# First and last runs of four graph layers: feature rows streamed past 32 loaded weights in four column tiles, a spread row and bounds in registers

## What is computed

```python
def reference(x, src, dst, edge_attr_16, edge_weight, ...):
    x = layernorm(x + L0(x, edge_attr_16, src, dst))    # softmax over the edges of a dst
    x = layernorm(x + L1(x, src, dst, edge_weight))     # softmax again, then an MLP of two 64-128-64 products
    x = layernorm(x + L2(x, row=src, col=dst))          # sums by src, gathers from dst, degrees as weights
    x = layernorm(x + L3(x, row=src, col=dst, value=edge_weight))
    return x

# L0, L1:  h = segment_sum(alpha[:, None] * f(x[src]), dst, num_segments=N)
# L2, L3:  h = segment_sum(weight[:, None] * x[dst], src, num_segments=N)
```

## Time and profile before

| what | value |
|---|---|
| median of 3 runs | 2804.57 us (2801.99 to 2814.03) |
| span of the profiled execution | 2797.4 us |
| mean granted clock of PE, as a share of full speed | 0.815 |
| busy: PE, DVE, POOL, ACT | 1944.0, 1685.3, 1661.4, 1497.3 us |

### The profile page before, as it was taken

The page is one execution under the profiler, slowest core; times in us unless marked ns, Lnnn a source line. Parts: engine busy times, 40 slices in busy tenths (PEclk is TensorE's granted clock), DMA queues, the critical chain, the costliest instruction groups (busy, mean ns, idle before and its releaser), DMA issues. The chain is left out here.

```text
span 2797.4 us, 27574 instructions
## 1 busy us (share of the span) xinstructions
PE 1944.0 (69%) x8422; PEld 1002.8 (36%) x8422; DVE 1685.3 (60%) x3220; ACT 1497.3 (54%) x2242; POOL 1661.4 (59%) x1610
## 2 busy tenths in 40 slices
PE   6998778679988688888999868658888875000000
PEld 3444334227643233364444327543333434000000
DVE  4876699993888578745655433997656687000002
ACT  4777667553677568746787762337777652000000
POOL 6777777600037565000777757775777768677774
PEclk9999899886999789979999996559989885555555
DMA  3233222101668674102454491442111233100002
GB/s 63 66 68 81 58 56 68 51 30 45 203 126 58 47 56 52 46 16 71 139 144 137 118 228 53 120 121 67 52 52 53 89 105 98 55 17 22 22 21 96
DMA packets 235785, 214.75 MB, mean 77 GB/s; under 512 B 156783, under 2 KB 169926, under 8 KB 235638
## 3 DMA queue, kind: packets, MB, share of 16 engines
q1 hardware_dynamic: 181190, 166.34, 20.7%
q0 software_dynamic: 51200, 46.31, 12.2%
q10 hardware_dynamic: 3248, 0.34, 0.1%
HBM read 140.36 MB, written 86.04 MB: 81 GB/s over the span
## 5 line engine op out<-in xcount | busy, mean ns | idle before, releaser
L2372 POOL DMA_INDIRECT stab<-wk,rank_i x200 | 208.5, 1042 | 289.1 <-DVE wk L588 231.4
L545 ACT ACTIVATE b_s<-ps,vec 128x512 f32<-128x512 f32 (+1 forms) x356 | 240.9, 684 | 159.4 <-PE ps L624 59.8
L2369 POOL DMA_INDIRECT u<-x2tab,dpos_i x200 | 220.8, 1104 | 82.7 <-issue 77.8
L2369 POOL DMA_INDIRECT u<-x3tab,src_i x200 | 206.1, 1030 | 85.3 <-issue 59.2
L2369 POOL DMA_INDIRECT u<-in_x_dram,src_i x200 | 201.4, 1007 | 76.7 <-issue 59.8
L2369 POOL DMA_INDIRECT e_b<-x0tab,dpos_i x72 | 72.7, 1009 | 290.9 <-DVEq L2174 265.5
L2372 POOL DMA_INDIRECT out_dram<-u,dst_i x176 | 198.2, 1126 | 74.7 <-issue 59.8
L2369 POOL DMA_INDIRECT u<-in_x_dram,dst_i x200 | 201.1, 1006 | 64.4 <-issue 59.5
L2372 POOL DMA_INDIRECT out_dram<-u,sfin_i x200 | 196.5, 982 | 66.3 <-issue 66.3
L776 DVE TENSOR_SCALAR b_x<-b_s 128x8 f32<-128x8 f32 x2 | 0.3, 168 | 389.3 <-DMA b_gl<-out_dram 389.3
L533 PE MATMUL ps<-b_h,blk_c 128*128 128x512 f32 (+1 forms) x296 | 174.4, 673 | 57.9 <-ACT b_gl L553 57.4
(11 more groups left out here) (428 smaller groups left out, 5026.4 us busy)
## 6 DMA issues: line engine op xcount, KB each, us to landing
b_gl<-in_x_dram SPq DMA_DIRECT2D x98, 256.0 KB, 2.7
wk<-dlist SPq DMA_DIRECT2D x50, 500.0 KB
wk<-slist SPq DMA_DIRECT2D x50, 500.0 KB
out_dram<-b_gl SPq DMA_DIRECT2D x93, 256.0 KB, 2.0
u<-stab SPq DMA_DIRECT2D x25, 510.0 KB
x2none<-b_gl SPq DMA_DIRECT2D x25, 250.0 KB
wk<-x2none SPq DMA_DIRECT2D x25, 240.0 KB
x2tab<-wk SPq DMA_DIRECT2D x25, 240.0 KB
```

What stands on the lines that cost most here:

```text
L545: return nc.scalar.activation(b_s[l][:, 0:w], pB[l][:, 0:w], ACT.Abs_reciprocal_sqrt, bias=col(EPSV))
L2369: pool.indirect_dma_start(out=o, out_offset=None, in_=tab, in_offset=at_ix(ix), **kw).then_inc(s, 16)
L2372: pool.indirect_dma_start(out=tab, out_offset=at_ix(ix), in_=a, in_offset=None, bounds_check=rows_n - 1, oob_is_err=False).then_inc(s, 16)
```

## The change

**Sums.** The operands change places. `hw` is now what is loaded: the four columns of the eight blocks of a group, 32 columns, and the 512 feature columns of that group stream past them. The result is 32 x 512, of which only an eighth is wanted (columns of `hw` of a block against features of the same block). Four groups make a chunk: their four matmuls write the partitions 0, 32, 64 and 96 of one PSUM bank, `e0` and `e1` in turn. There are 7 chunks, the last of one group. For each chunk DVE multiplies the bank by a mask of the wanted blocks (`mask8`), reduces the eight blocks to one (into `q_b`), PE transposes that (L1454 of the changed kernel), and DVE copies it out and gives the bank back. So a layer has 25 matmuls of 512 streamed columns and 7 transposes on PE, and 21 instructions of DVE more, in place of 100 or 200 matmuls; the scan now runs over one piece in layer 1 too and its copies out of PSUM fall away. In layer 0 columns 2 and 3 of `hw` are set to zero. In layer 3 chunk c waits for the gathers of its last groups.

**Spread row.** `x0tab` gets 1024 rows behind row E in place of one, all filled with the bias row, and the index of a source without an incoming edge becomes E + 8p, where p is the partition of the index's place in the layout in which the indices are made.

**Bounds.** The two bounds of POOL's DMAs are put in registers once.

Two semaphores are merged into others, with their counts (`list_st`, `consts`).

```diff
+    NONE = 8
-    x0tab, ... = (dram(n, (r, D)) for n, r in (("x0tab", E + 1), ...))
+    x0tab, ... = (dram(n, (r, D)) for n, r in (("x0tab", E + 128 * NONE), ...))
...
-        e_a, e_b, e_c, e_d, q_a, q_b = (sb(n, [128, 512]) for n in ("e_a", "e_b", "e_c", "e_d", "q_a", "q_b"))
+        e_a, e_d, q_a, q_b = (sb(n, [128, 512]) for n in ("e_a", "e_d", "q_a", "q_b"))
+        e_bc = sb("e_bc", [128, 1024])
+        e_b, e_c = e_bc[:, 0:512], e_bc[:, 512:1024]
...
         def ends_unit(layer, after, **deps):
-            us = (.14 if layer < 2 else .23) * GC
...
+            text = []
+            for c in CHUNKS:
+                b = f"e{c % 2}"
+                text += [f"p{c} pe 1.6 +{b}" + (f" <p{c - 1}" if c else ""), f"m{c} dve .7 <p{c}", f"r{c} dve .7 <m{c}",
+                         f"x{c} pe .3 <r{c}", f"y{c} dve .25 -{b} <x{c}"]
+            text += ["scan dve {}".format((2.9, 5.0, 2.3, 2.3)[layer]), "t pe 1 +e1", "copy dve .5 -e1"]
+            unit(("lay", layer), 0, ";".join(text), after, **deps)
...
+            if m == 0:
+                nc.vector.memset(hw[0:P, :, 2:4], 0.0)
...
         def ends_pe(pe, t, layer):
-            def block(b):
-                return nc.tensor.matmul(e0[0:D, k * b:k * b + k], a[0:P, b, :], hw[0:P, b, 0:k], start=True, stop=True)
-            def pair(b):
...
+            a = (xs, xs, rdst, rdst)[layer]
+            for c in CHUNKS:
+                yield t[f"p{c}"]
+                bank_c, name = chunk_bank(c)
                 pe.wait_ge(S("weights"), layer + 1)
+                pe.wait_ge(S(name + "_free"), use(name, t[f"p{c}"]))
+                if layer == 3:
+                    for g in chunk_groups(c)[-2:]:
+                        pe.wait_ge(*gathered(3, g))
+                for q, g in enumerate(chunk_groups(c)):
+                    last_e = nc.tensor.matmul(bank_c[32 * q:32 * q + 32, :],
+                                              hw[0:P, GC * g:GC * g + GC, :].rearrange("p b k -> p (b k)"),
+                                              a[0:P, GC * g:GC * g + GC, :], start=True, stop=True)
                 last_e.then_inc(S("ends_ps"), 1)
+        def ends_rows_pe(pe, t, layer):
+            for c in CHUNKS:
+                yield t[f"x{c}"]
+                r = 32 * len(chunk_groups(c))
+                pe.wait_ge(S("ends_red"), len(CHUNKS) * layer + c + 1)
+                nc.tensor.transpose(chunk_bank(c)[0][0:D, 0:r], q_b[0:r, D * c:D * c + D], ident[0:r, 0:r]).then_inc(S("ends_t"), 1)
+        def ends_mask_dve(dve, t, layer):
+            for c in CHUNKS:
+                yield t[f"m{c}"]
...
+                product = (q_a, e_d)[c % 2]
+                k = stepped(nc.vector.tensor_tensor(t3(product[0:r, :]), t3(chunk_bank(c)[0][0:r, :]), bc(mask8[0:r, :], D), ALU.mult))
+                yield t[f"r{c}"]
+                dve.wait_ge(S("dve_step"), k)
+                nc.vector.tensor_reduce(q_b[0:r, D * c:D * c + D], product[0:r, :].rearrange("p (b d) -> p d b", b=GC), AX.X,
+                                        ALU.add).then_inc(S("ends_red"), 1)
+        def ends_copy_dve(dve, t, layer):
...
+                dve.wait_ge(S("ends_t"), len(CHUNKS) * layer + c + 1)
+                nc.vector.tensor_copy(ends_sums(layer)[0:D, 32 * k * c:32 * k * c + n * k].rearrange("d (b k) -> d b k", k=k),
+                                      bank_c[0:D, 0:4 * n].rearrange("d (b k) -> d b k", k=4)[:, :, 0:k]).then_inc(S(name + "_free"), 1)
...
-            stt(addr, addr, -float(E), valid, ALU.add, ALU.mult)
-            ts(addr, addr, float(E), None, ALU.add)
+            none_row = sgn[:, 15:16]
+            ts(none_row, X["io"][:, 0:1], NONE / 128.0, float(E), ALU.mult, ALU.add)
+            stt(addr, addr, none_row, valid, ALU.subtract, ALU.mult)
+            ts(addr, addr, none_row, None, ALU.add)
...
-            sp.dma_start(x0tab[E:E + 1, :], rowc[0:1, R_B0, :]).then_inc(S("x0_none"), 16)
+            sp.dma_start(x0tab[E:E + 128 * NONE, :].rearrange("(p s) d -> p s d", s=NONE),
+                         rowc[:, R_B0, :].unsqueeze(1).broadcast_to((128, NONE, D))).then_inc(
+                S("x0_none"), 16)
...
+            last_edge, last_node = pool.to_reg(E - 1), pool.to_reg(N - 1)
-            def gather(o, tab, ix, s, rows_n=None):
-                kw = {} if rows_n is None else dict(bounds_check=rows_n - 1, oob_is_err=False)
+            def gather(o, tab, ix, s, last=None):
+                kw = {} if last is None else dict(bounds_check=last, oob_is_err=False)
...
+            fours = stepped(nc.vector.tensor_reduce(wpn[:, 0:32], ident[:, :].rearrange("p (a k) -> p a k", k=4), AX.X, ALU.add))
+            dve.wait_ge(S("dve_step"), fours)
+            nc.vector.tensor_reduce(mask8[:, :], wpn[:, 0:32].rearrange("p (g b) -> p b g", b=GC), AX.X, ALU.add)
```

More of the change, by code:

```diff
@@ L49, in gnn_resnorm_kernel @@
         dram(n, (FLAT,)) for n in ("q_spos", "q_ddeg", "q_dps", "q_sdeg", "q_dpos", "q_rank"))
-    x0tab, x2tab, x2none, x3tab = (dram(n, (r, D)) for n, r in (("x0tab", E + 1), ("x2tab", E), ("x2none", E), ("x3tab", E)))
+    x0tab, x2tab, x2none, x3tab = (dram(n, (r, D)) for n, r in (("x0tab", E + 128 * NONE), ("x2tab", E), ("x2none", E), ("x3tab", E)))
     stab = dram("stab", (E, RW))
@@ L1415, in softmax_dve, with chunk_bank, chunk_groups @@
             dve.drain().then_inc(S("weights"), 1)
+        def chunk_bank(c):
+            return (e0, e1)[c % 2], f"e{c % 2}"
+        def chunk_groups(c):
+            return range(4 * c, min(4 * c + 4, NG))
         def ends_pe(pe, t, layer):
-            a, k = (xs, xs, rdst, rdst)[layer], (2, 4, 2, 2)[layer]
-            def block(b):
-                return nc.tensor.matmul(e0[0:D, k * b:k * b + k], a[0:P, b, :], hw[0:P, b, 0:k], start=True, stop=True)
-            def pair(b):
-                o, c = (e1, b - QB) if k == 4 and b >= QB else (e0, b)
-                return nc.tensor.matmul(o[:, k * c:k * c + 2 * k], xs[0:P, b:b + 2, :].rearrange("p b d -> p (b d)"),
-                                        hw[0:P, b:b + 2, 0:k], start=True, stop=True)
@@ new lines, in ends_copy_dve @@
+        def ends_copy_dve(dve, t, layer):
+            k = 4 if layer == 1 else 2
+            for c in CHUNKS:
+                yield t[f"y{c}"]
+                n = GC * len(chunk_groups(c))
+                bank_c, name = chunk_bank(c)
+                dve.wait_ge(S("ends_t"), len(CHUNKS) * layer + c + 1)
+                nc.vector.tensor_copy(ends_sums(layer)[0:D, 32 * k * c:32 * k * c + n * k].rearrange("d (b k) -> d b k", k=k),
+                                      bank_c[0:D, 0:4 * n].rearrange("d (b k) -> d b k", k=4)[:, :, 0:k]).then_inc(S(name + "_free"), 1)
@@ L2412, in _ @@
                 for k in range(GC):
-                    scatter(stab, E, rank_i[:, GC * g + k:GC * g + k + 1], rec[g % 2][:, RW * k:RW * k + RW], S(f"placed{g % 2}"))
+                    scatter(stab, last_edge, rank_i[:, GC * g + k:GC * g + k + 1], rec[g % 2][:, RW * k:RW * k + RW], S(f"placed{g % 2}"))
             pool.wait_ge(S("x2_st"), 32 * NG)
@@ L2429, in _ @@
                 for b in range(GC * g, GC * g + GC):
-                    gather(rdst[:, b, :], x3tab, spos_i[:, b:b + 1], gathered(3, g)[0], E)
+                    gather(rdst[:, b, :], x3tab, spos_i[:, b:b + 1], gathered(3, g)[0], last_edge)
             for l in LANES:
@@ L2444, in _ @@
                         rows, ix = rdst[:, b, :] if g >= STAGED else staged(g)[:, D * k:D * k + D], fidx_i
-                    scatter(out, N, ix[:, b:b + 1], rows, S("final_st"))
+                    scatter(out, last_node, ix[:, b:b + 1], rows, S("final_st"))
         @block.tensor
@@ L2453, in _ @@
             pe_programs += [softmax_pe(pe, at["sm", m], m) for m in range(2)]
-            pe_programs += [ends_pe(pe, at["lay", layer], layer) for layer in range(4)]
+            pe_programs += [p(pe, at["lay", layer], layer) for p in (ends_pe, ends_rows_pe) for layer in range(4)]
             pe_programs += [carry_pe(pe, at["lay", layer], layer) for layer in range(4)]
@@ L2501, in _ @@
             dve_programs += [softmax_dve(dve, at["sm", m], m) for m in range(2)]
-            dve_programs += [carry_dve(dve, at["lay", layer], layer) for layer in range(4)]
+            dve_programs += [p(dve, at["lay", layer], layer) for p in (ends_mask_dve, ends_copy_dve, carry_dve) for layer in range(4)]
             dve_programs += [prep2_dve(dve, at["prep2", k], k) for k in range(2)]
```

90 lines of the change are left out of this document (26 added, 64 removed).

## The result

The changed kernel takes **2760.57 us** (median of 4 runs, 2747.97 to 2764.01) against 2803.28 us of the kernel before beside it: a ratio of 0.9835 with a 95% interval of 0.9806 to 0.9863. The forecast was 2765, range 2705 to 2825. The profiled execution has a span of 2760.7 us against 2797.4, so -36.7 us. The sum came out near the forecast (-36.7 us for -40); several of its terms did not.

What follows compares the result with a forecast made beforehand. POOL's gathers and scatters bound the kernel from 1326 us on, PE and its chain before that. Terms -8 -12 +4 -5 -11 -6 -2 sum to -40 us, a span of 2757; with 7.2 for the median, 2765 us, range 2705 to 2825.

Steps and rivals of the forecast that it cites:

- stab scatters: First stab scatter to x2tab gathers: second record stands 17 DVE instructions behind the first instead of 13, POOL waits; +4 us.
- Layer 0's sums: Layer 0's sums up to the x0tab gathers: cheaper chunks against more dense work and PE waits; -8 us (-13 to +11).
- x0tab to second softmax: First x0tab gather to second softmax: spread row quickens gathers, added dense work refills the room; 381 to 365 us, -16.
- PE reaches 92 to 96% where it leads: x0tab gathers to second softmax: 343 us of PE work divided by 0.94 gives 365 us.
- Layer 1: Second softmax to first stab scatter: softmax +7, sums -8, way to the first record +5 us.
- Layer 2 and the x3tab gathers: Layer 2: shorter sums before the store POOL waits for, -5 us; x3tab gathers: less DVE time beside them, -2 us.
- The own wait: POOL's 14.5 us gap inside the last scatters falls to about 4, as dense blocks before layer 3's last sums leave; -11.
- The next scatters: 89 scatters in the 139.6 us after that gap: four dense blocks leave, about a quarter of the DVE time; -6 us.
- Registers: Bounds of POOL's DMAs: 1000 register moves go, but they were hidden; 0 us (bounds 0 and -38).
- The slow one: Rival, chance 0.15: column tiles run one after another at PE's low clock, 93 us more, total 2858.
- More than that: Rival, chance 0.20: register moves cost 0.04 us each (-38), or x0tab stretch falls by 46 us at full clock; about 2730.
- The dense blocks eat the gain: Rival, chance 0.18: x0tab stretch stays at 381 us, softmax and first record take upper prices; 2793 us, no change.

Runs made afterwards that it cites:

- the long hold: Changed kernel with no new dense block started from the first x0tab gather to layer 1's second group: 2635.37 us, ratio 0.9421.
- the short hold: Changed kernel with no new dense block started between the second softmax and layer 1's second group: 2721.74 us, ratio 0.9723.

## Why the prediction was right, and where its steps were not

The total was right partly by luck, since errors cancel: the sums of layers 0 and 1 gave 25 us more than forecast, and the x0tab stretch, the way to the first record, the stab scatters and the last scatters came out 32 us worse. The 7.2 us added for the median over the span did not come either: the median, 2760.57 us, lies at the span of the profiled execution, 2760.7.

- **Layer 0's sums** (-8, measured -21.6). The chunk was right (1.00 us for 1.2), the transposes too (2.0 us for 2.1). Two other terms were mis-sized. The 4 us charged for PE's waits on DVE did not come: PE is busy 22.65 of 22.80 us, the dense matmuls between the chunks cover the chain through DVE. And the other work, reckoned as 4.5 us as before plus 15.8 us, took 13.3 us in the first row of the table, with PE's busy time in the second about as before (122.91 against 123.80): two dense matmuls there had cost 3.8 us at the low clock, and now all run at the full one, where one behind another of its shape takes 0.86 us and not the 1.10 us priced. The clock was in the prediction, but only as a sign to look for, not as a term. The price of a tile change, put at nothing, is about 0.1 us each and is part of the 1.00 us of a chunk.
- **x0tab to second softmax** (-16, measured -9.7). The mechanism was right on both sides: the row gives 25 to 33 us, and the refill takes some 24 us of it back. The step that failed is "PE reaches 92 to 96% where it leads": it was busy 328.30 of 373.4 us, 88%, and the work itself was 15 us less than the 343 us reckoned. The run with the long hold shows what the dense blocks cost there: 105 us of PE's busy time went (328.30 to 223.21), and with it 98 us of the stretch.
- **Layer 1** (softmax +7, sums -8, first record +5; measured +4.4, -19.4, +13.5). The sums are the same error as in layer 0. The first record was charged by DVE instructions, up to +12; the hold showed that the dense blocks which start in softmax and sums are the cause.
- **stab scatters** (+4, bounds 0 to +8; measured +15.8). Right in place, too small: the second record alone costs 9 us (20.4 us behind the first, 11.4 before), the rest of the scatters 3 us, and the start of the x2tab gathers another 3.
- **Layer 2 and the x3tab gathers** (-5 and -2; -4.2 and -3.3): right in size. Layer 2's sums fell from 45.5 to 24.4 us, most of it hidden by POOL's gathers; the wait fell by 9.2 us, from 21.5 to 12.3, but the x2tab gathers ahead of it took 289.4 us instead of 284.4. In the run with the bounds as numbers, of the same order, they took 284.8, so these 5 us may be scatter between runs. In the x3tab gathers the mechanism is the one named: DVE's busy time fell from 160.79 to 132.55 us, the gathers above 1.1 us from 18 to 12, and POOL's busy time from 206.09 to 202.95 us.
- **The own wait** (-11, measured -12.7): right, and so is its reason: the last sums now end at 2180.7 us, 3.5 us after POOL's last x3tab gather, where they had ended 15 us after it.
- **The next scatters** (-6, measured -0.7). This step failed. DVE's busy time did fall (113.54 to 89.96 us, as the earlier trace rows and the last row of the table show), but 88 scatters kept POOL busy for 115.05 us, where 89 had for 112.74. POOL and DVE side by side in the changed kernel:

```profile
2282.88 1.25 POOL L2385 DMA_INDIRECT out_dram<-u,dst_i  x1 [0.30 <-issue]
2284.39 1.19 DVE L988 TENSOR_TENSOR wk<-wk,vcs 127x1000 f32<-127x1000 f32 x1
2284.43 2.01 POOL L2385 DMA_INDIRECT out_dram<-u,dst_i  x1 [0.30 <-issue]
...
2290.71 0.98 POOL L2385 DMA_INDIRECT out_dram<-u,dst_i  x1 [0.30 <-issue]
2290.89 0.69 DVE L1652 TENSOR_REDUCE vsum<-e_d 125x8 f32<-125x512 f32 x1 [0.69 <-ACT e_d L1663]
```

The scatter at 2284.43 us takes 2.01 us; it lies beside L988, DVE's comparison of equal nodes (127 x 1000, both inputs in SBUF). All 21 scatters of 2.0 us in this stretch overlap an L988. The 22 others above 1.1 us overlap L996, L1636 or L1655, products that also read two operands from SBUF. Of the 45 that take 0.98 us, 23 overlap no DVE work, 11 the reduction L1652 alone, one L1648, which reads PSUM and SBUF, and 10 an L1655. That is layer 3's own work; no step of a dense block stands beside them. Before, too, each of the 38 scatters above 1.1 us overlapped a step of layer 3's groups, and the ten of 2.0 us the same comparison (L981). The Trainium skill ("SBUF — State Buffer", SBUF: two separate sides) says that a DVE operation with two SBUF inputs and a GpSimd operation that reads SBUF hold one port pair in turn, whole instructions long; the scatter takes its indices, `dst_i`, from SBUF. The trace agrees where L988 is concerned: 0.98 us alone, 2.01 beside a comparison of 1.19 us; the 10 that L1655 left alone don't follow from it.
- **Registers** (0): right.
- **Rivals.** The slow one fell with the chunk of 1.00 us. "More than that" was wrong in its reasons: register loads cost nothing, and the x0tab stretch did not come down to POOL's pace though PE's clock there rose from 0.88 to 0.93. "The dense blocks eat the gain" was half right: they did, in three places, but not all of it. That the change and the order together are the larger prize was not among the rivals: with new dense blocks kept out of one part of the program the changed kernel gains some 116 us more (ratio 0.9421 for 0.9835), while the same hold gives the kernel before nothing (0.9980).

## What to carry to other kernels

Work without a deadline that fills the gaps of a chain makes the chain as long as the filler allows: when a step of the chain is made cheaper, look at what the scheduler puts into the place, and hold it out where another engine waits for the chain's end. Check that the filler has room behind: in the kernel before the same hold only moved the wait to the last scatters (57.0 us). Small matmuls are worth turning round so that the few columns are loaded and the many are streamed, and four column tiles of 32 then cost about one matmul (1.00 us together, 3.55 us one after another). Before charging a contention to an engine's total busy time, find the instructions that the slow ones overlap.

## What was unexpected in the hardware

The clock. In the runs with the long and with the short hold the sums of layer 1 stood alone on PE, without dense matmuls between them, and they ran at different clocks. In the run with the long hold PE was busy 12.22 of 27.4 us in the softmax ahead, at a granted clock of 0.66, and 15.71 of 24.6 us in the sums, at 0.50; a chunk took 1.94 us and came every 3.02 us:

```profile
1099.67 1.94 PE L1444 MATMUL ps<-u,hw 125*32 125x512 f32 x8 [0.73 <-DVE e_bc L1480]
1101.54 0.42 PE L1454 MATMUL ps<-ident,q_b 128*64 128x128 f32 x1
1102.69 1.94 PE L1444 MATMUL ps<-u,hw 125*32 125x512 f32 x8 [0.73 <-DVE e_bc L1480]
```

In the run with the short hold, behind a busier softmax (23.23 of 33.2 us, at 0.90), a chunk took 1.06 us at 0.87, every 2.15 us. Both paces are set by the chain chunk, mask, reduction, transpose, copy, in which two banks take turns. And the one hot row had no fixed cost: the 200 gathers took 296.3 us before, 294.0 us before with the long hold and 274.7 us in the changed kernel with the long hold and one row, against 255.9 us with the row spread. What makes the difference between the last two figures with one row is open.
